# A head's squares on ScalarE and their sums on VectorE instead of six GpSimd operations, and layer two's output weights split during the projections

## What is computed

```python
attn1 = softmax(q1 @ k1.T * scale) @ v
attn2 = softmax(q2 @ k2.T * scale) @ v
attn = attn1 - lambda_full * attn2                    # 16 heads of 32 columns
rms = rsqrt(mean(attn * attn, axis=-1) + 1e-5)        # per token and head
attn = attn * rms * subln_w * (1.0 - LAMBDA_INIT)
x = layernorm(x + attn.reshape(b, t, 512) @ wo.T)
```

## Time and profile before

| | us |
|---|---|
| median of three runs | 2494.23 |
| the three runs | 2489.93, 2494.23, 4612.64 |
| the profiled execution | 2488.43 |
| its span, first to last instruction | 2486.7 |
| TensorE busy | 2348.2 (94%) |
| VectorE busy | 1622.7 (65%) |
| ScalarE busy | 1215.6 (49%) |
| GpSimd busy | 390.2 (16%) |
| mean granted TensorE clock | 0.972 of full speed |

### The profile page before, as it was taken

The page is one execution under the profiler, slowest core; times in us unless marked ns, Lnnn a source line. Parts: engine busy times, 40 slices in busy tenths (PEclk is TensorE's granted clock), DMA queues, the critical chain, the costliest instruction groups (busy, mean ns, idle before and its releaser), DMA issues. The chain is left out here.

```text
span 2486.7 us, 43820 instructions
## 1 busy us (share of the span) xinstructions
PE 2348.2 (94%) x15600; PEld 1333.0 (54%) x15600; DVE 1622.7 (65%) x3725; ACT 1215.6 (49%) x2390; POOL 390.2 (16%) x797
## 2 busy tenths in 40 slices
PE   6999999999999999899999999978999999888989
PEld 5663333333333333478888888856444443333367
DVE  2357888888888887364444444443688887777567
ACT  2126666666666666442222212331466665555634
POOL 3000010000100101320000000000123232222262
PEclk9999999999999999899999999988999999898999
DMA  5663321232222200110000000016412212210011
GB/s 194 160 137 79 64 27 27 33 46 28 27 27 27 27 2 2 31 52 19 10 23 25 25 25 25 1 44 151 90 22 40 41 29 33 40 21 2 2 39 55
DMA packets 58031, 109.11 MB, mean 44 GB/s; under 512 B 11820, under 2 KB 23084, under 8 KB 57832
## 3 DMA queue, kind: packets, MB, share of 16 engines
q1 hardware_dynamic: 56248, 100.25, 19.9%
q0 software_dynamic: 1584, 6.29, 0.7%
HBM read 73.75 MB, written 31.46 MB: 42 GB/s over the span
## 5 line engine op out<-in xcount | busy, mean ns | idle before, releaser
L617 ACT ACTIVATE l_w_hi_prob<-l_p_work 128x512 f32<-128x512 f32 (+3 forms) x1792 | 870.9, 552 | 440.1 <-PE l_p_work L519 417.6
L669 DVE TENSOR_REDUCE l_maxima<-l_p_ring 128x1 f32<-128x512 f32 x1280 | 805.9, 683 | 129.2 <-PE l_p_ring L497 120.1
L539 PE MATMUL l_p_work<-l_w_hi_prob,v_all 128*32 128x512 f32 (+3 forms) x3584 | 817.5, 563 | 51.6 <-POOL l_w_hi_prob L469 51.4
L539 PE MATMUL l_p_work<-l_w_hi_prob,l_ones 128*32 128x512 f32 (+3 forms) x3584 | 817.5, 564 | 0.0
L519 PE MATMUL l_p_work<-xT_all 50*128 50x512 f32 (+3 forms) x1680 | 432.5, 414 | 0.0
L497 PE MATMUL l_p_ring<-xT_all 48*128 48x512 f32 (+3 forms) x1680 | 432.2, 415 | 0.0
L539 PEld LDWEIGHTS l_p_work<-l_w_hi_prob,v_all 128*32 128x32 f32 x3584 | 168.9, 110 | 380.2 <-issue 266.4
L497 PEld LDWEIGHTS l_p_ring<-xT_all 48*128 48x128 f32 x1680 | 219.4, 187 | 234.4 <-DVE l_maxima L669 155.8
L666 DVE CUSTOM_DVE_ANT_0 l_masked_scores<-l_p_ring,l_mask 128x128 bf16<-128x128 f32 (+3 forms) x512 | 241.6, 487 | 118.9 <-PE l_p_ring L497 109.7
L519 PEld LDWEIGHTS l_p_work<-xT_all 50*128 50x128 f32 x1680 | 225.3, 188 | 168.6 <-ACT l_w_hi_prob L617 89.0
L469 POOL TENSOR_SCALAR_AFFINE_SELECT l_w_hi_prob<-l_w_hi_prob 128x256 f32<-128x256 f32 x256 | 104.7, 421 | 528.4 <-ACT l_w_hi_prob L617 528.3
(11 more groups left out here) (155 smaller groups left out, 3210.6 us busy)
## 6 DMA issues: line engine op xcount, KB each, us to landing
xT_all<-q_parts SPq DMA_DIRECT2D x180, 128.0 KB
q_parts<-l_part SPq DMA_DIRECT2D x64, 256.0 KB
xT_all<-k_parts SPq DMA_DIRECT2D x90, 128.0 KB
k_parts<-l_part SPq DMA_DIRECT2D x40, 256.0 KB
xT_all<-k_parts SPq DMA_DIRECT2D x90, 64.0 KB
x<-in_x_T SPq DMA_DIRECT2D x4, 1024.0 KB, 10.9
x<-in_L_attn_x POOLq DMA_DIRECT2D x1, 4096.0 KB, 15.7
ffn_w<-in_L_ffn_gate_w_T SPq DMA_DIRECT2D x8, 512.0 KB, 3.6
```

What stands on the lines that cost most here:

```text
L539: summing = pe.matmul(p_out[r0:r0 + VD, off:CH], lhs, prob[step % PRING][:, sub, off:CH], start=first, stop=final)
L617: act.activation(prob[step % PRING][:, sub, off:CH], p_score[:, at % SCORE_BANKS, off:CH], ACT.Exp, scale=HD ** -0.5).then_inc(exped, 1)
L669: dve.tensor_reduce(to, scores, AX.X, ALU.max).then_inc(freed, 1)
```

## The change

Three things change.

1. `square(n)` leaves GpSimd. ScalarE makes the squares with one activation (`Square`, 128x256) in the middle of head n + 1 in L1, of head n + 2 in L0, behind the first exponential of the middle step. VectorE sums them with one `tensor_reduce` (`average(n)`), behind the `keep` of head n + 1's second query half. There is one buffer `squares`, so that ScalarE also waits for `averaged`.
2. `prepare_wo` of L1 runs on GpSimd at the start of the phase, as soon as all the input weights are split, ahead of all selects. In L0 its twelve steps stand together in GpSimd's order and start when the first sixteen heads are summed.
3. The load of L1's output weights moves from GpSimd's queue in L1 to SP's queue at the start of `ffn_phase`.

```diff
-            def square(n):
-                ...
-                pool.tensor_tensor(squares[:, :, :], head, head, ALU.mult).then_inc(squared, 1)
-                for i in range(1, HALVINGS):
-                    ...
             def prepare_wo(step):
 
                 k, what = divmod(step, 3)
-                if step == 0:
+                if step > 0:
+                    pool.wait_ge(wo_ready, step)
+                elif loads:
                     pool.wait_ge(loaded, 16 * len(loads))
-                elif step > 0:
-                    pool.wait_ge(wo_ready, step)
+                    pool.wait_ge(summed, HEADS // 2 * S)
...
+            if not loads:
+                pool.wait_ge(split_lo, len(jobs))
+                for step in range(3 * KD):
+                    prepare_wo(step)
             for n in range(HEADS):
...
-                if n:
-                    square(n - 1)
-                if HEADS // 2 < n <= HEADS // 2 + 3 * KD:
+                if loads and HEADS // 2 < n <= HEADS // 2 + 3 * KD:
                     prepare_wo(n - HEADS // 2 - 1)
-                if n == 1:
+                if loads and n == 1:
...
-            square(HEADS - 1)
...
+            def square(n):
+
+                tiles = attn[:, :].rearrange("p (t c) -> p t c", c=D)
+                rows = slice((n // NH) * KT, (n // NH + 1) * KT)
+                act.wait_ge(out_kept, QC * (n + 1))
+                if n:
+                    act.wait_ge(averaged, n)
+                act.activation(squares[:, :, :], tiles[:, rows, (n % NH) * VD:(n % NH + 1) * VD], ACT.Square
+                               ).then_inc(squared, 1)
...
+            behind = 1 if L.causal else 2
...
+                if at % (2 * S) == S and at >= 2 * S * behind:
+                    square(at // (2 * S) - behind)
+            for n in range(HEADS - behind, HEADS):
+                square(n)
...
+            def average(n):
+                rows = slice((n // NH) * KT, (n // NH + 1) * KT)
+                dve.wait_ge(squared, n + 1)
+                dve.tensor_reduce(mean_sq[:, rows, n % NH:n % NH + 1], squares[:, :, :], AX.X, ALU.add).then_inc(averaged, 1)
+
...
                     keep(*at)
+                    if at[1] == QC - 1 and at[0]:
+                        average(at[0] - 1)
+            average(HEADS - 1)
...
+            qkv1_loads.append((wo_stage, by_k(A["L1_attn_Wo_T"])))
...
-                            [(wo_stage, by_k(A["L1_attn_Wo_T"]))])
+                            early_q[:, :, :], early_k[:, :, :], mean_sq, wo, norm_w[:, 1:2], [])
```

More of the change, by code:

```diff
@@ L61 @@
 LAST_LAG = 6
-HALVINGS = VD.bit_length()
 MIX_WRITTEN_OUT = 8
@@ L299, in attention_phase @@
         out_recip, out_kept = sem("out_recip"), sem("out_kept")
-        loaded, squared, wo_ready = sem("loaded"), sem("squared"), sem("wo_ready")
+        loaded, squared, averaged, wo_ready = sem("loaded"), sem("squared"), sem("averaged"), sem("wo_ready")
         squares = w_area.taken_by("squares", [P, KT, VD], F32, PRING * 2 * CH + 2 * CH + 2 * QPC * VD)
@@ L430, in _ @@
                         pool.tensor_tensor(xT.lo[at], x_stage[at], xT.hi[at], ALU.subtract).then_inc(pool_lo, 1)
-            def square(n):
[L433 to L436, removed]
-                if n:
-                    pool.wait_ge(squared, HALVINGS * n)
-                pool.tensor_tensor(squares[:, :, :], head, head, ALU.mult).then_inc(squared, 1)
-                for i in range(1, HALVINGS):
[L441 to L445, removed]
             def prepare_wo(step):
                 k, what = divmod(step, 3)
-                if step == 0:
+                if step > 0:
+                    pool.wait_ge(wo_ready, step)
+                elif loads:
                     pool.wait_ge(loaded, 16 * len(loads))
-                elif step > 0:
-                    pool.wait_ge(wo_ready, step)
+                    pool.wait_ge(summed, HEADS // 2 * S)
                 if what == 0:
@@ L1413, in program @@
             attention_phase(nc, L1, xT, q_parts[1], k_parts[1], v_sb, attn_area, 2 * H_SIZE, neg_lambda[1][:, 0:1], C,
-                            early_q[:, :, :], early_k[:, :, :], mean_sq, wo, norm_w[:, 1:2],
-                            [(wo_stage, by_k(A["L1_attn_Wo_T"]))])
+                            early_q[:, :, :], early_k[:, :, :], mean_sq, wo, norm_w[:, 1:2], [])
             early.close()
```

## The result

The changed kernel takes 2413.33 us in the median (2410.03 to 2414.65), against 2492.08 us (2489.82 to 2494.23) for the kernel before on the same chip: a ratio of 0.9683, with a 95% interval of 0.9661 to 0.9704. One of the four executions of each kernel (10356.81 and 4612.64 us) was disturbed: it counts in these two medians (without it they are 2412.01 and 2489.93) but in neither the ranges nor the ratio. The profiled execution took 2410.03 us (span 2408.3), against 2488.43: 78.4 us less.

A forecast was written before the change was run, and what follows sets the result against it. TensorE bounds L0; in L1 its sums wait for GpSimd's selects and the clock dips. Savings 22.4 + 47.2 + 2.9 + 2.4 = 74.9, less 3, give 72: 2416 profiled, plus 2, 2418 us; range 2405 to 2440.

The forecast's parts named there:

- The wait behind GpSimd goes entirely: L1, sixteen intervals behind head 1: TensorE's sums no longer wait for GpSimd's selects, saving 22.4 us.
- the 16.7 to 16.8: Sign of being right: intervals between two heads of L1 of 16.7 to 16.8 us, the same for heads 17 to 28.
- The clock dips come from the longer waits: L1, twelve later intervals: clock returns to full as waits go, saving 47.2 us, of which 26.1 waiting and 21.1 clock.
- The last heads 2.9 us, the ends 2.4: L1's last heads lose 2.9 us of waiting; shorter operations at each layer's end save 1.2 us, 2.4 in both.
- The rival that the dips stay: L1's twelve later heads give back only 26.1 us, dips having another cause: 2439 us, chance 0.09.
- ScalarE's squares cost nothing: Squares of about 0.39 us on ScalarE in both layers, hidden by its idle time: no cost.
- the slower rival: ScalarE reloads the activation table at each `Square` and the exponential behind it: 54 us slower, 2544 us, chance 0.02.
- VectorE's sum brings 3 us into the ring: L1: the new 0.4 us sum delays the ring of four banks by 0.1 us a head, costing 3 us.
- the rival in which TensorE pays for both operations: Bank rings are tight in both layers; each head pays 0.39 + 0.4 us: 2464 us, chance 0.08.
- L0's thirty intervals: Sign of being right: L0's thirty intervals from its head 1 on together still take 782.7 us.
- The output weights during the projections: nothing: L1's twelve steps, at most 15.1 us, fit GpSimd's 108.14 us idle ahead of its first select: no cost.
- the addition of 2 us for the median: Added to the 2416 us expected of a profiled execution to forecast the median, 2418 us.

The follow-up runs named there:

- filler6: Changed kernel with six 128x128 multiplications on unrelated data put on GpSimd behind each head's last select in L1: 2499.78 us.
- Experiments 1 and 3: 1: changed kernel, L1's output-weight steps and load back in their old places, 2410.93 us; 3: kernel before, L1's steps behind heads 3 to 14, 2489.73 us.
- experiment 8: Changed kernel with unrelated 128x128 multiplications on GpSimd behind each head's last select in L1: six, 2499.78 us; eight, 2583.65 us.
- experiment 7: Changed kernel with ScalarE making each head's squares three times, twice into a spare tile: 2413.46 us.
- experiment 5: Kernel before, with squares and output-weight steps of L1 both moved on GpSimd behind a head's fourth select: 2416.74 us.
- experiment 6: Changed kernel with VectorE making each head's sum of squares three times, 2430.02 us, or twice, 2421.82 us.
- both_mid: The kernel of experiment 5: kernel before, L1's squares and output-weight steps on GpSimd behind a head's fourth select: 2416.74 us.
- experiment 2: Kernel before, with L1's output-weight steps made during the projections and their load on SP's queue, squares left on GpSimd: 2455.41 us.
- weights_only: The kernel of experiment 2: kernel before, only L1's output-weight steps and their load moved, squares left on GpSimd: 2455.41 us.
- squares_mid: Kernel before, with GpSimd keeping the squares but making them in L1 behind the next head's fourth select: 2415.40 us.
- squares_only: Changed kernel with L1's output-weight steps back behind heads 17 to 28 on GpSimd and their load behind head 1: 2410.93 us.

## Why the prediction was right

The forecast was 2418 us in a range of 2405 to 2440; it is 2413.33. Step by step:

- **The wait behind GpSimd goes entirely (22.4 us for sixteen intervals).** It was 23.6. The difference is TensorE's own time for a head, 16.60 and not the 16.68 that busy time over intervals had given: as I read it, the busy time of the stretch with waits held 0.08 us a head that wasn't work. The heads of filler6 without a dip bear it out: 18.35 - 16.60 is 0.08 more than their wait of 1.67. So the intervals lie 0.1 us below the 16.7 to 16.8 that the prediction named as a sign. The room of 1.1 us fits the waits read at this place. The work there less the wait of TensorE: 2.40 - 1.34 = 1.06 (squares), 2.40 + 1.26 - 2.57 = 1.09 (with a weights' step), 1.28 - 0.17 = 1.11 (a long step alone), 2.78 - 1.67 = 1.11 (six fillers), 3.73 - 2.62 = 1.11 (eight). Behind head 30 the wait is 0.2 us longer in each of these kernels that has one.
- **The clock dips come from the longer waits (21.1 of 47.2 us for twelve intervals).** It was 48.2 in all. Experiments 1 and 3 rule out the place in the run, and experiment 8 makes dips with work that has nothing in common with the old one but its engine and its place. The rival that the dips stay, 2439, falls.
- **The last heads 2.9 us, the ends 2.4.** They gave 2.7 and 2.8 (1.47 and 1.36). From the end of L0's last `keep` to the table load it was 3.05 us with the six old operations and is 1.58 with the three new ones.
- **ScalarE's squares cost nothing.** Right, by experiment 7. They take 0.43 us and not 0.39. The Trainium skill, "ScalarE: Activation LUTs", section "What ACT_TABLE_LOAD costs", led to an estimate of 399 ns; the row has 427, so it is 7% too small here, and nothing hangs on it. No table load stands beside a `Square`, and ten loads remain ten, so that the slower rival (2544) falls, and the rule of that page's section "Table sets: the hidden batching unit" does not bite: the trace shows the exponential and `Square` under one loaded table.
- **VectorE's sum brings 3 us into the ring.** This was the mis-sized term: it brought nothing (experiment 5). I had compared its 0.4 us with a single gap of 0.29 us. The sum occupies 0.33 us, and the operations behind it close up to one another: VectorE is busy 238.18 / 16 = 14.89 us a head, where I had reckoned 15.26. But experiment 6 shows that only 0.06 us was left, and that every further sum would cost 0.3 us a head. The mechanism was there, just beyond the edge. In both_mid, which has no sum on VectorE, it is busy 14.71 us in heads that also take 16.60, so that the sum adds 0.18 to it. With it falls the rival in which TensorE pays for both operations (2464); L0's thirty intervals took 783.0 us, against 782.7 before.
- **The output weights during the projections: nothing.** The twelve steps took 11.3 us, from 1649.82 to 1661.12, and the first select of L1 came behind a long idle time (answers to rows 11):

```profile
1755.53 0.41 POOL L457 TENSOR_SCALAR_AFFINE_SELECT l_w_hi_prob<-l_w_hi_prob 128x256 f32<-128x256 f32 x1 [94.41 <-ACT l_w_hi_prob L612]
```

The terms that the change sets gave 77.4 us and not 72: 2.2 of the difference are TensorE's 0.08 us a head, 3 the ring, the rest the ends and the last heads. The profiled execution was forecast at 2416 and took 2410.03; the addition of 2 us for the median was 3.3.

What the prediction did not say is how the two parts divide. It put the weights' steps among the causes of 26.1 + 21.1 us. In fact their move is worth nothing that these runs can tell once the squares are gone (2410.93 without, 2413.33 with it), since steps of 0.6 and 0.7 us fit into the room of 1.1 and those of 1.28 cost 0.24 us a head, four times. Nothing that was run is measurably faster than the changed kernel.

## What to carry over

When one engine stands in a chain for each head (here exponential, select, sum), read how much other work fits between two of its links, and compare each piece of side work at that place with the room: here 2.4 us stood in 1.1, while 4.5 us of idle time lay on the same engine some places earlier in its order. Moving the work in the order gave what moving it to other engines gave. Where TensorE's waits are long enough for the granted clock to fall, count what the clock costs as well, and don't add the worth of two edits that shorten the same wait.

## What the runs showed of the hardware

**The clock follows the length of the waits.** With 1.34 us of waiting in each head of 18.0 us there was no dip in 28 heads in a row (experiment 2). With 1.67 us 11 of 28 heads had one, and the kernel's runs spread by 15 us. With 1.9 to 2.6 us, behind heads 17 to 28 of the kernel before, the mean clock was 0.90. With 2.62 us every head had one. What of a wait decides, its length or what stands around it, these runs don't separate.

**GpSimd slowed VectorE down in L0.** VectorE's last operation of `keep` in L0's heads, in the kernel before:

```profile
L706 DVE SCALAR_TENSOR_TENSOR attn<-l_w_hi_half,neg_lambda 128x128 f32<-128x128 f32 x60 | 27.8, 463 | 2.1
```

and in the changed kernel:

```profile
L706 DVE SCALAR_TENSOR_TENSOR attn<-l_w_hi_half,neg_lambda 128x128 f32<-128x128 f32 x60 | 21.1, 352 | 2.1
```

It reads two operands from SBUF, and took 463 ns on average instead of 352. The average hides two values. Around the squares of one head, in the kernel before:

```profile
601.69 0.35 DVE L706 SCALAR_TENSOR_TENSOR attn<-l_w_hi_half,neg_lambda 128x128 f32<-128x128 f32 x1
602.81 1.49 POOL L444 TENSOR_TENSOR l_w_hi_squares<-l_w_hi_squares 128x128 f32<-128x128 f32 x4
602.85 0.57 DVE L706 SCALAR_TENSOR_TENSOR attn<-l_w_hi_half,neg_lambda 128x128 f32<-128x128 f32 x1
```

Of the 64 such operations in L0 the 31 that run at the same time as GpSimd's halving additions take 570 to 581 ns, and the other 33 take 352. weights_only, squares_mid and both_mid, which keep L0's squares on GpSimd, show the same two groups; in the changed kernel and in squares_only, where they are gone from it, all 64 take 352. It isn't the data: in filler6 two of these operations ran beside a multiplication on GpSimd that shares nothing with them, and took 442 and 444 ns. A select on GpSimd alone did nothing (352 ns beside 30 of them in L1, before), and VectorE's row maxima out of PSUM (L675 in filler6) took 685 ns with a multiplication beside them and without. It cost no time here, as VectorE is not the bound in L0. The Trainium skill, "GPSIMD Engine Reference", section "1. Specifications", says that GpSimd's SBUF interfaces are shared with VectorE, and that an instruction of VectorE with two inputs from SBUF contends for them; the trace agrees in that the operation slowed has two such inputs.
